# Macaron block with a gated-slot-attention layer: the second and third tap of the values' convolution moved directly behind the last merge on VectorE

## What is computed

```python
q, k = short_conv(h @ Wq, cq), short_conv(h @ Wk, ck)      # 16 heads of 128
v, w = short_conv(h @ Wv, cv), short_conv(h @ Ww, cv)      # 4 taps in time, then SiLU
w = l2norm(w); g = sigmoid(h @ Wf1 @ Wf2); beta = sigmoid(h @ Wb)
# per step t, with bw = beta_t * w_t:
Sk = Sk * g_t + k_t (outer) bw          # state 128 x 128
Sv = Sv * g_t + bw (outer) v_t
o_t = softmax(q_t @ Sk * scale) @ Sv
# then RMS norm, gate, @ Wo, residual
```

## Time and profile before

| | |
|---|---|
| median of 3 runs | 2809.45 us (2808.47 to 2810.02) |
| the profiled execution | 2808.98 us, span of its trace 2807.1 us |
| PE busy | 2757.3 us (98%) |
| PEld busy | 1933.3 us (69%) |
| DVE busy | 2229.9 us (79%) |
| ACT busy | 1671.3 us (60%) |
| POOL busy | 1425.0 us (51%) |
| mean DMA traffic | 53 GB/s over the span |

### The profile page before, as it was taken

The page is one execution under the profiler, slowest core; times in us unless marked ns, Lnnn a source line. Parts: engine busy times, 40 slices in busy tenths (PEclk is TensorE's granted clock), DMA queues, the critical chain, the costliest instruction groups (busy, mean ns, idle before and its releaser), DMA issues. The chain is left out here.

```text
span 2807.1 us, 43427 instructions
## 1 busy us (share of the span) xinstructions
PE 2757.3 (98%) x13814; PEld 1933.3 (69%) x13814; DVE 2229.9 (79%) x5777; ACT 1671.3 (60%) x3777; POOL 1425.0 (51%) x2122
## 2 busy tenths in 40 slices
PE   7999999999999999999999999999999999999999
PEld 5887566666666666666666666666666666666887
DVE  7554588988888899888888888888889888884543
ACT  5111677677777677776777677677677777760110
POOL 0200466666566666665666666656666666660000
PEclk9999999999999999999999999999999999999999
DMA  4500211111112111111121111111212111105000
GB/s 169 195 16 28 66 36 35 35 50 35 50 35 69 52 57 35 50 35 49 35 72 50 57 35 51 33 50 35 72 51 60 35 50 38 51 24 199 15 16 30
DMA packets 90932, 151.06 MB, mean 54 GB/s; under 512 B 9297, under 2 KB 30929, under 8 KB 90193
## 3 DMA queue, kind: packets, MB, share of 16 engines
q1 hardware_dynamic: 90704, 148.29, 16.8%
HBM read 127.02 MB, written 21.23 MB: 53 GB/s over the span
## 5 line engine op out<-in xcount | busy, mean ns | idle before, releaser
L1552 PE MATMUL ps<-hT,space 128*128 128x512 f32 x2048 | 996.1, 594 | 1.1 <-ACT hT L1023 1.1
L902 POOL TENSOR_TENSOR s<-s,tmp 128x256 f32<-128x256 f32 (+1 forms) x448 | 367.2, 820 | 302.7 <-DVE tmp L1219 281.4
L1552 PEld LDWEIGHTS ps<-hT,space 128*128 128x128 f32 x2048 | 345.9, 191 | 194.8 <-issue 167.6
L902 POOL TENSOR_TENSOR X<-S,D 128x256 f32<-128x256 f32 x384 | 275.9, 718 | 108.6 <-ACT S L1077 82.5
L1596 PEld LDWEIGHTS ps<-Y,S 128*128 128x128 f32 x1536 | 220.8, 191 | 151.3 <-issue 133.7
L333 ACT ACTIVATE sig<-up_ps 128x512 f32<-128x512 f32 x88 | 52.7, 599 | 406.7 <-PE up_ps L542 406.5
L542 PE MATMUL up_ps<-h_hi,wq 128*128 128x512 f32 x704 | 281.1, 399 | 2.2 <-DVE h_lo L404 2.1
L1584 PEld LDWEIGHTS ps<-AM,XT 128*128 128x128 f32 x1536 | 216.5, 191 | 94.6 <-issue 90.1
L902 POOL TENSOR_TENSOR Y<-aT,D 128x256 f32<-128x256 f32 x384 | 280.5, 752 | 0.0
L542 PE MATMUL up_ps<-h_lo,wq 128*128 128x512 f32 x704 | 278.3, 395 | 0.0
L902 POOL TENSOR_TENSOR A<-ident,dg 128x512 f32<-128x512 f32 x64 | 66.6, 1041 | 390.0 <-DVE space L1296 384.2
(11 more groups left out here) (187 smaller groups left out, 6383.2 us busy)
## 6 DMA issues: line engine op xcount, KB each, us to landing
space<-in_wk_dram SPq DMA_DIRECT2D x64, 256.0 KB, 2.6
space<-in_ww_dram SPq DMA_DIRECT2D x64, 256.0 KB, 2.6
space<-in_wq_dram SPq DMA_DIRECT2D x64, 256.0 KB, 2.7
space<-in_wv_dram SPq DMA_DIRECT2D x64, 256.0 KB, 2.7
space<-in_wo_dram SPq DMA_DIRECT2D x64, 256.0 KB, 3.2
wq_dram<-wq SPq DMA_DIRECT2D x3, 2816.0 KB, 19.4
space<-in_w_dram SPq DMA_DIRECT2D x8, 704.0 KB, 10.9
x_sb<-in_x_dram SPq DMA_DIRECT2D x4, 1024.0 KB, 5.4
```

The costliest lines, as they stand in the source:

```text
L902: return nc.gpsimd.tensor_tensor(out, in0, in1, op)
L1552: mm = nc.tensor.matmul(bank[x][:, :], ck_(slot[x], kk), hT[n // NH % 2][:, kk, :], start=(kk == 0), stop=(kk == KT - 1))
```

## The change

The two taps cv2 and cv3 move ahead of p8, p16 and p32 on DVE. The list of steps is changed accordingly, the wait for cv1 is written out, and the value's SiLU on ACT no longer implies p32, so ACT gets a wait for it of its own ahead of h64.

```diff
-DVE_EARLY = ("ck1 ck2 ck3 cw1 cw2 cw3 p2 cq1 ss cq2 p4 cq3 cv1 p8 p16 cv2 p32 cv3 kr p64 As at0 at1 at2 at3 "
+DVE_EARLY = ("ck1 ck2 ck3 cw1 cw2 cw3 p2 cq1 ss cq2 p4 cq3 cv1 cv2 cv3 p8 p16 p32 kr p64 As at0 at1 at2 at3 "
@@ ScalarE, turn(u)
                     act.wait_ge(dve_early, after(DVE_EARLY, "cv3", n))
                     silu_folded(v, "v")
+                    act.wait_ge(dve_early, after(DVE_EARLY, "p32", n))
                     keep_decays(64)
@@ VectorE, turn(u)
                     merge(64)
                 if early:
+                    dve.wait_ge(dve_early, after(DVE_EARLY, "cv1", n))
+                    conv("v", 2)
+                    dve.wait_ge(dve_early, after(DVE_EARLY, "cv2", n))
+                    conv("v", 3)
                     dve.wait_ge(dve_early, after(DVE_EARLY, "p4", n))
                     decays(4)
                     dve.wait_ge(act_early, after(ACT_EARLY, "h8", n))
                     dve.wait_ge(dve_early, after(DVE_EARLY, "p8", n))
                     decays(8)
-                    conv("v", 2)
                     dve.wait_ge(act_early, after(ACT_EARLY, "h16", n))
                     dve.wait_ge(dve_early, after(DVE_EARLY, "p16", n))
                     decays(16)
-                    dve.wait_ge(dve_early, after(DVE_EARLY, "cv2", n))
-                    conv("v", 3)
                     dve.wait_ge(pe_early, after(PE_EARLY, "kT", n))
```

## The result

The changed kernel takes 2835.68 us (median of 4 runs, 2834.26 to 2838.34) against 2809.70 us (median of 4, 2808.47 to 2810.02) for the kernel before on the same chip: a ratio of 1.0098, 95% interval 1.0086 to 1.0110. It is 26.0 us slower. The forecast was 2838 with a range of 2822 to 2866. The profiled execution took 2834.83 us, with a span of 2833.0.

What follows compares the result with a forecast made beforehand. PE was taken to bound the kernel; 59 turns x 0.43 = 25.4, plus 4 x 0.79 = 3.2, plus 0.5 for the first turn, sum to 29.1 us on 2808.98: 2838 us, range 2822 to 2866.

Steps and rivals of the forecast that it cites:

- What bounds the kernel: Attention layer: PE, busy 2188.32 of 2200 us at clock 1.00, bounds; DVE is next with 1921.39 us.
- Earlier taps bring nothing: ACT's SiLU starts directly behind c32, not waiting for cv3, so cv3 coming 1.28 us earlier gains 0.
- p8 was said to start at 6.14: On DVE, p8 starts at 6.14 instead of 4.70, takes 0.41, and is done 1.23 us later.
- The road b8, c16, b16, c32, b32, b64, X: Across POOL and ACT, late p8 makes c32 and b64 0.79 us later, reaching PE's transposes of X.
- the slack ahead of osq: On ACT, osq waits for PE until 7.35, holding c32 back today; in the new order b16 binds c32.
- The no-change rival: Idle times of POOL, ACT and PE take up the 1.23, b64 ends before 11.97: 2809; chance 0.09.
- a wait of 0.43 us a turn: PE at the transposes of X: 0.79 late less 0.36 of slack, over 59 turns 25.4 us.
- b8 was taken at 0.81: On POOL, b8 starts at 6.62, 0.07 behind p8, keeps its 0.81 and ends at 7.43; bounds 0.62 and 1.00.
- b32 to b64 was taken as fixed at 2.63: On POOL, b32 to b64 stays 2.63, filled by r2 to r5 and b64, so b64 ends at 12.37.
- The first four: Turns u = 0 to 3, where PE already waits for v and X: whole delay counts, 4 x 0.79 = 3.2 us.
- DVE's lateness behind kr: On DVE, kr holds oss up by 0.2 to 0.4; `on` and later steps move some 0.5 us, not reaching PE.
- The rival of full blocking: DVE decays and POOL products wait each other out wholly: c32 1.34 later, 0.98 a turn, 2872; chance 0.12.

Runs made afterwards that it cites:

- the extra instruction: Changed kernel plus one unused instruction of a tap's size on DVE between cv2 and cv3: 2875.31 us, ratio 1.0237 against the kernel before.
- The runs without the power: Power in r4 on GpSimd replaced by a product: changed kernel 2846.11 us, also with the residual ahead of am1 2823.31 us; kernel before, as control, 2806.68 us.

## Why the prediction was right, and where its sizes were off

**Right, step by step.** What bounds the kernel (PE without a gap) held: its clock is at 1.00 in the turns from the sixth on and its instructions are unchanged. Earlier taps bring nothing: the SiLU runs 0.32 behind c32 as before, and making it really early gave 2835.88. p8 was said to start at 6.14 and to end at 6.55; it started at 1016.00 - 9.87 = 6.13 and ended at 6.55. The road b8, c16, b16, c32, b32, b64, X is the one that the rows show, the slack ahead of osq is used up, and the distance of 0.14 to 0.15 between the end of b64 and X held in every run in which PE waited there. The run with one tap ahead shows the slack, the extra instruction the one-for-one cost beyond it. The no-change rival (the idle times take it up) is true only for half the change.

**Sizes.** Predicted was a wait of 0.43 us a turn, measured 0.35 to 0.36. Two terms were off and nearly cancel, so that the total came within 3 us of the measured one is in part luck.
- b8 was taken at 0.81 and took 0.91, behind a handover that took 0.14 instead of 0.07. So c32 was late by 18.68 - 9.87 - 7.84 = 0.97 instead of 0.79.
- b32 to b64 was taken as fixed at 2.63 and took 2.38. r4 fell from 1.15 to 1.01 us and r2 followed b32 sooner. So b64 ended 0.72 late instead of 0.79, and 0.72 - 0.36 gives the 0.36. Why the power is shorter was not tested.

In the 59 turns this makes 21 us instead of 25.4. The first four cost 4.6 instead of 3.2. Some 2 of that come from a lower clock (below), which was not in the sum; without it they are 2.5 to 2.7, since the turns grew by 0.61 to 0.66 and not by the 0.79 that was taken as the whole delay. PE's busy time was to stay near 2757 us and rose to 2770.8: the waits that the busy time hides had been overlooked.

**What was taken too lightly.** DVE's lateness behind kr was put at 0.2 to 0.4 and at "some 0.5" for `on` and what follows, and called harmless because PE moves too. kr was 0.58 late, the residual and `on` 0.71 to 0.72, while PE moved by 0.35. It cost nothing only because the slack at the first scores was 0.86. The runs without the power found this second gate by walking into it.

**The rival of full blocking** (2872) did better at b8 than the forecast. It had b8 end at 7.63, c16 start at 7.66 and b16 at 8.16; measured were 7.60, 7.64 and 8.13, where the forecast had 7.43, 7.46 and 7.96. It failed one step later: it had p64 start near 8.1, ahead of b16, and hold it up to 9.15. p64 started at 8.51, behind b16, which took 0.65 as before; so c32 was 0.97 late and not 1.34, and the turn 0.35 longer and not 0.98. In kind the rival was right elsewhere too: b64 beside am1, p64 beside b16, b64 beside a diagonal product each stretched DVE's instruction by 0.24 to 0.43 us. The Trainium skill, page "SBUF — State Buffer", section "Who interferes with whom", names the condition, two operands from SBUF on VectorE against a reading instruction on GpSimd; the runs agree, since the residual, with one of its operands in PSUM, was not stretched in the same place. That the first one keeps the ports for the whole instruction, as the prediction has it, the page says outright only of VectorE's two-port modes; the runs show nearly that for this pair too (last section).

## What to carry to other kernels

Before moving work ahead of an instruction, follow not who consumes the moved work but who waits for what it is moved past, across all engines to the one that bounds, and count the slack there; half a move may be free and the whole one not. When a wait is taken away and the time does not fall, compare starts of the bounding engine from one instruction to the next: the waits table hides any wait shorter than the modelled drain. And an instruction shifted in time also gets a new neighbour on the other engine, which here was worth as much as the wait removed.

## What the runs showed of the hardware

In these runs a DVE instruction with both operands in SBUF that starts just behind a reading POOL instruction is held up until that one is nearly through: 0.83 instead of 0.42 us (am1, 0.08 behind b64) and 0.72 instead of 0.29 (a diagonal product, 0.04 behind b64). Counted back from their ends by what they take alone, both began 0.14 to 0.15 before the recorded end of b64. The residual, which reads one operand from PSUM, stays at 0.69, 0.08 behind b64.

In the first turns PE waits longest for v (up to 2.4 us in the changed kernel), and behind two of these waits the granted clock fell in the trace. The window of the changed kernel that holds the fourth interval, columns as in the earlier trace rows:

```profile
422.00:458.50 36.50, 33.90 (x172) 23.96 (x171) 31.53 (x87) 24.53 (x56) 21.75 (x32) 0.93 0.11 33
```

A mean of 0.93 between the two levels (1.2 and 2.4 GHz) means that PE ran at the lower one for about 14% of that stretch. Narrower windows show where: the clock is at 0.50 from 420.40, behind the wait for v that ended at 419.16, and again from 454.60, at the end of the next one (454.76). The fourth interval took 36.4 us, where the run with the early SiLU, without such a drop, took 34.51: some 1.9 us. In the kernel with the extra instruction it happened in two intervals (0.92 in each, 37.28 and 36.88 us). PE had waited for v in each of these turns, 2.4 us in the changed kernel and 2.9 in the other. But such a wait does not always do it: the changed kernel waited 2.41 in the turn before as well, and the run with the early SiLU waited up to 2.4 (for As) in the same turns, both at a clock of 1.00. So waits of a few microseconds can have a price beyond their length, in some executions. That this is why the times of some of the slower kernels lie 3 to 5 us apart is likely, but was not tested.
